# The next batch's turned x: loaded from DRAM and normalised along its columns, instead of turned on TensorE

## The reference

```python
x = x + jnp.tanh(g_xattn[0]) * xattn(_layernorm(x, axis=-1), ctx_1024, ctx_1024, Wq, Wk, Wv, Wo)
x = x + jnp.tanh(g_ffn[0]) * ffn(_layernorm(x, axis=-1), router_w, w1, w2)

def _layernorm(x, axis=-1, eps=1e-05):
    m = jnp.mean(x, axis=axis, keepdims=True)
    v = jnp.var(x, axis=axis, keepdims=True)
    return (x - m) / jnp.sqrt(v + eps)
```

## Time and profile before

| | us |
|---|---|
| median of three runs | 1805.26 (1804.03 to 1808.17) |
| the profiled execution | 1803.87 |
| its span, first to last instruction | 1802.1 |
| PE busy | 1687.2 (94%) |
| DVE busy | 1418.2 (79%) |
| ACT busy | 1288.7 (72%) |
| POOL busy | 539.6 (30%) |

### The profile page before, as it was taken

The page is one execution under the profiler, slowest core; times in us unless marked ns, Lnnn a source line. Parts: engine busy times, 40 slices in busy tenths (PEclk is TensorE's granted clock), DMA queues, the critical chain, the costliest instruction groups (busy, mean ns, idle before and its releaser), DMA issues.

```text
span 1802.1 us, 31795 instructions
## 1 busy us (share of the span) xinstructions
PE 1687.2 (94%) x10074; PEld 905.6 (50%) x10074; DVE 1418.2 (79%) x2293; ACT 1288.7 (72%) x3653; POOL 539.6 (30%) x821
## 2 busy tenths in 40 slices
PE   8999999999999989999999998888899999999997
PEld 5223333333333323333333332214899999999997
DVE  7999999999999999999999999997444444444442
ACT  5999999999999999999999999997111111111111
POOL 3331252352243225235223422213222222222222
PEclk9999999999999999999999999999999999999999
DMA  8546225513711731461272163319322222222222
GB/s 233 127 126 179 70 65 143 148 40 104 199 46 51 189 97 47 133 182 40 76 192 62 59 158 88 134 69 297 92 36 38 35 35 37 36 38 35 35 36 28
DMA packets 128247, 172.90 MB, mean 96 GB/s; under 512 B 14496, under 2 KB 105760, under 8 KB 128128
## 3 DMA queue, kind: packets, MB, share of 16 engines
q1 hardware_dynamic: 113152, 150.51, 30.4%
q0 software_dynamic: 14144, 20.44, 6.5%
q10 hardware_dynamic: 832, 0.53, 0.1%
HBM read 117.96 MB, written 53.47 MB: 95 GB/s over the span
## 4 chain that ended last, share of the span: by engine, by line
PE 37%; ACT 26%; DVE 20%; issue 10%; POOL 4%; DMA 2%; SPq 0%; POOLq 0%; DVEq 0%; ACTq 0%
ACT w_all L921 24%; DVE negmax L1102 14%; PE scores L1495 14%; PE scores L1508 13%; PE scores L724 3%; PE acc L737 3%; POOL routed_rows L1302 2%; DVE resid L997 1%; ACT w_all L866 1%; PE spare L587 1%; DMA out<-row_t,gate_token 1%; POOL vz L1325 1%; PE spare L581 1%; DVE rz L1088 1%; PE spare L1485 1%
## 5 line engine op out<-in xcount | busy, mean ns | idle before, releaser
L921 ACT ACTIVATE w_all<-scores,negmax 128x512 f32<-128x512 f32 (+1 forms) x1664 | 1127.6, 751 | 24.3 <-DVE negmax L1102 18.7
L1102 DVE TENSOR_REDUCE negmax<-scores 128x2 f32<-128x1024 f32 (+1 forms) x832 | 1002.6, 1216 | 63.9 <-PE scores L724 56.2
L724 PE MATMUL scores<-q_stack,w_all 128*128 128x512 bf16 (+1 forms) x1664 | 501.4, 383 | 49.9 <-ACT w_all L921 47.8
L921 ACT ACTIVATION_READ_ACCUMULATOR w_all<-scores,negmax 128x1 f32 (+1 forms) x1664 | 449.0, 270 | 0.0
L737 PE MATMUL acc<-w_all,vz 128*32 128x512 f32 (+1 forms) x3328 | 443.2, 605 | 3.0 <-POOL vz L1325 2.8
L1541 ACT ACTIVATE projections<-scores 128x512 f32<-128x512 f32 x142 | 84.9, 598 | 445.0 <-PE scores L1495 445.0
L724 PEld LDWEIGHTS scores<-q_stack,w_all 128*128 128x128 bf16 (+1 forms) x1664 | 115.3, 99 | 524.5 <-ACT w_all L921 391.9
L1325 POOL TENSOR_TENSOR vz<-w_all,rz 128x68 f32<-128x68 f32 (+1 forms) x416 | 125.2, 301 | 787.8 <-DVE rz L1088 762.1
L1495 PEld LDWEIGHTS scores<-row_t,q_stack 128*128 128x128 f32 x2272 | 264.4, 192 | 6.8 <-issue 1.9
L1495 PE MATMUL scores<-row_t,q_stack 128*128 128x128 f32 x2272 | 265.6, 275 | 1.7 <-DVE row_t L1568 1.7
L1508 PE MATMUL scores<-room,projections 128*128 128x256 f32 x1136 | 256.8, 379 | 0.0
(11 more groups left out here) (215 smaller groups left out, 1044.0 us busy)
## 6 DMA issues: line engine op xcount, KB each, us to landing
w_all<-k_parts SPq DMA_DIRECT2D x248, 200.1 KB, 3.5
w_all<-in_w SPq DMA_DIRECT2D x16, 1024.0 KB, 10.0
q_stack<-q_parts SPq DMA_DIRECT2D x248, 64.0 KB, 3.2
k_parts<-parts SPq DMA_DIRECT2D x42, 300.0 KB, 2.8
w_all<-in_ctx_t SPq DMA_DIRECT2D x7, 1601.0 KB
parts<-routed SPq DMA_DIRECT2D x71, 129.0 KB
q_parts<-parts SPq DMA_DIRECT2D x14, 384.0 KB, 3.5
routed<-pad_row SPq DMA_DIRECT2D x8, 645.0 KB
```

The costliest lines, as they stand in the source:

```text
L724: mm = pe.matmul(scores[0:r, 2 * (u % SLOTS) + j % 2, :], k_stacks[g][:, j, lt * P:lt * P + r], q_stack[:, g, j, :], start=True, stop=True)
L921: e = act.activation(probs[0:r, s % RING, j, :], scores[0:r, 2 * (u % SLOTS) + j % 2, :], ACT.Exp, bias=negmax[0:r, u % 4, j % 2:j % 2 + 1 ...
L1102: dve.tensor_reduce(negmax[0:r, u % 4, :], scores[0:r, 2 * (u % SLOTS):2 * (u % SLOTS) + 2, :], AX.X, ALU.max, negate=True).then_inc(negma ...
```

## The change

The host gives the kernel x a second time, with channels in rows (`in_x_t`), and SP loads a batch of it into `x_t` (for batch 1 at the start, later for the batch after next, behind part q 1). The statistics are still taken by DVE from `x_in`. Behind the inverse deviation, SP stores the mean and the inverse deviation of the 512 tokens into a small DRAM tensor (`x_stats`, 2 x 512), waits for both to land, and loads its 4 KB into every partition, over `x_in`, whose rows aren't wanted any more. POOL subtracts and multiplies in `x_t` itself, a half of the channels at a time, now in steps 20 to 23. The fills `x_turn` of steps 27 and 28 are gone, in batch 0's table too; batch 0's own x is still turned as before. `x_in` is reloaded when POOL has finished.

```diff
-    27: ("next", "x_turn", 0), 28: ("next", "x_turn", 1), 29: ("cur", "o_turn", 1), 31: ("next", "q", 0),
+    29: ("cur", "o_turn", 1), 31: ("next", "q", 0),
...
+SHIFT_X = 20
...
+    x_turned = x_t_in.rearrange("b (k p) n -> b p k n", p=P)
+    x_stats = room[:, 0, :].rearrange("p (s n) -> p s n", s=2)
...
+        def spread_x_stats(it):
+            b = it.b
+            sp.wait_ge(rstd_step, 2 * (b + 2))
+            for s, stat in ((0, mv1[:, :, 0]), (1, rstd1[:, 1, :])):
+                sp.dma_start(x_stats_dram[s].rearrange("(t p) -> p t", p=P), stat, allow_slow_non_contiguous=True).then_inc(x_stats_stored, 16)
+            wait_apart(sp, x_stats_stored, 32 * (b + 1), passed_sp)
+            sp.dma_start(x_stats[:, :, :], x_stats_dram.partition_broadcast(P)).then_inc(x_stats_in, 16)
+
         def load_x(it):
 
-            sp.wait_ge(fill_taken, it.made("x_turn", 1))
+            sp.wait_ge(xn_ready, 2 * (it.b + 2))
             sp.dma_start(x_in[:, :, :], x_rows[it.b + 2]).then_inc(x_loaded, 16)
...
+            sp.wait_ge(early_ready, EARLY.index(("q", 1)) + 1)
+            sp.dma_start(x_t[:, :, :], x_turned[1]).then_inc(x_t_loaded, 16)
...
                 for c in ORDER[0:KCHUNK]:
+                    if b == 0 and c == KC + KCHUNK - 1:
+                        spread_x_stats(it)
                     store_parts(it, c)
...
                 for c in ORDER[KCHUNK:2 * KCHUNK]:
+                    if b > 0 and c == KC + KCHUNK + 1:
+                        spread_x_stats(it)
                     store_parts(it, c)
...
                 store_parts(it, 1)
+                if it.ahead:
+                    sp.wait_ge(fill_ready, it.made("q", 1))
+                    sp.dma_start(x_t[:, :, :], x_turned[b + 2]).then_inc(x_t_loaded, 16)
...
-            if name == "x_turn":
-
-                pe.wait_ge(xn_ready, 2 * (b + 2))
-                mm = turn_x(spare, i)
-            elif name == "q":
+            if name == "q":
+                if i == 0 and 0 in halves:
+                    pe.wait_ge(xn_ready, 2 * (b + 2))
                 mm = project_q(spare, i, halves)
...
-            elif name == "x_turn":
-                act.wait_ge(fill_ready, it.made(name, i))
-                act.copy(x_t[:, i, :], spare[:, :]).then_inc(fill_taken, 1)
...
-                if it.next and s in (CENTRE_X, CENTRE_X + 1):
-                    by_row(ALU.subtract, x_in, x_in, mv1[:, :, 0], s - CENTRE_X).then_inc(centred1, 1)
-                if it.next and s in (CENTRE_X + 2, CENTRE_X + 3):
+                if it.next and s in (SHIFT_X, SHIFT_X + 1):
+                    k = s - SHIFT_X
+                    if k == 0:
+                        wait_apart(pool, x_t_loaded, (b + 1) * 16, passed_pool)
+                        pool.wait_ge(x_stats_in, (b + 1) * 16)
+                    pool.tensor_tensor(x_t[:, k, :], x_t[:, k, :], x_stats[:, 0, :], ALU.subtract).then_inc(centred1, 1)
+                if it.next and s in (SHIFT_X + 2, SHIFT_X + 3):
+                    k = s - SHIFT_X - 2
                     pool.wait_ge(centred1, 2 * (b + 1))
-                    by_row(ALU.mult, x_in, x_in, rstd1[:, 1, :], s - CENTRE_X - 2).then_inc(xn_ready, 1)
+                    pool.tensor_tensor(x_t[:, k, :], x_t[:, k, :], x_stats[:, 1, :], ALU.mult).then_inc(xn_ready, 1)
```

More of the change, by code:

```diff
@@ L203, in rows_of, with attention_and_routing @@
     return min(P, L - lt * P)
-def attention_and_routing(nc, ctx, block, keep, x, ctx_t, g_xattn, g_ffn, wq_t, wk_t, wv_t, wo_t, router_t,
-                          w1, w2, out, routed, q_parts_dram, k_parts_dram):
+def attention_and_routing(nc, ctx, block, keep, x, x_t_in, ctx_t, g_xattn, g_ffn, wq_t, wk_t, wv_t, wo_t, router_t,
+                          w1, w2, out, routed, q_parts_dram, k_parts_dram, x_stats_dram):
     ident, tri, ones, pad_row, plan = (keep[name] for name in ("ident", "tri", "ones", "pad_row", "plan"))
@@ L356, in attention_and_routing @@
     centred1 = sem("centred1")
+    x_t_loaded = sem("x_t_loaded")
+    x_stats_stored = sem("x_stats_stored")
+    x_stats_in = sem("x_stats_in")
     centred2 = sem("centred2")
@@ L1113, in run @@
                     f = it.fill(s)
-                    if f and f[0] not in ("v", "own_v", "x_turn") and p == (f[0] in ("q", "k")):
+                    if f and f[0] not in ("v", "own_v") and p == (f[0] in ("q", "k")):
                         take(it, *f)
@@ L1627, in _, with flamingo_block @@
         pool.wait_ge(added, NBLK * 16)
-def flamingo_block(nc, x, ctx_t, g_xattn, g_ffn, wq_t, wk_t, wv_t, wo_t, router_t, w1, w2, out):
+def flamingo_block(nc, x, x_t, ctx_t, g_xattn, g_ffn, wq_t, wk_t, wv_t, wo_t, router_t, w1, w2, out):
     routed = nc.dram_tensor("routed", (SPARE + BLK, ROW), F32, kind="Internal").ap()
@@ L1633, in flamingo_block @@
     k_parts_dram = nc.dram_tensor("k_parts", (2, 3, D, L), BF16, kind="Internal").ap()
+    x_stats_dram = nc.dram_tensor("x_stats", (2, N), F32, kind="Internal").ap()
     with ExitStack() as ctx:
@@ L1642, in flamingo_block @@
         block = ctx.enter_context(nc.Block())
-        attention_and_routing(nc, ctx, block, keep, x, ctx_t, g_xattn, g_ffn, wq_t, wk_t, wv_t, wo_t, router_t, w1, w2,
-                              out, routed, q_parts_dram, k_parts_dram)
+        attention_and_routing(nc, ctx, block, keep, x, x_t, ctx_t, g_xattn, g_ffn, wq_t, wk_t, wv_t, wo_t, router_t, w1, w2,
+                              out, routed, q_parts_dram, k_parts_dram, x_stats_dram)
         experts(nc, ctx, block, keep, routed, out)
@@ L1658 @@
         ("x", np.ascontiguousarray(inputs["x"])),
+        ("x_t", turned(inputs["x"])),
         ("ctx_t", turned(inputs["ctx_1024"])),
```

## The result

The changed kernel takes 1860.13 us (median of 4 runs, 1858.83 to 1862.59) where the kernel before took 1805.36 beside it (4 runs, 1804.03 to 1808.17). The ratio is 1.0304, with a 95% interval of 1.029 to 1.0317: 3% slower, 55 us, far above the range. The profiled execution has a span of 1857.0 us.

A forecast was written before the change was run, and what follows sets the result against it. ACT and DVE were taken to bind at once beside the removed copies. A gain of 2.4 us, with the trip and other transfers at nought, took the median 1805.26 to 1802.9 (predicted 1803.0); range 1800.3 to 1811.5 us.

The forecast's parts named there:

- the landing of the second store: Statistics' trip through DRAM before step 20: landing 2.5 to 4.6 us after issue, 2.8 taken, in a trip of 7.3.
- Rival C: Statistics stores: 512 stores of 4 bytes twice take some 6 us instead of 2.8; 1810 and above; chance 0.08.
- Rival B: Load spreading 4 KB over 128 partitions: half rate, 3.1 us longer, trip 10.4 us, time 1809.9; chance 0.12.
- The room: POOL's wait at step 20: nothing lost up to a trip of 8.9 us after rstd; 7.3 expected, cost 0.
- The slope: POOL's wait at step 20: from a trip of about 9.4 us on, each microsecond costs one, seven times.
- The gain: Fills removed from steps 27 and 28: 0.3 us a batch for six batches plus 0.6 in batch 0, 2.4 us.
- rival A: Fills removed from steps 27 and 28: ACT alone binds, all 6.6 us arrive, time 1798.7; chance 0.11.
- rival D: Around 423 us: DVE gives nothing back, its waits being PE's own; time 1805.3; chance 0.17.
- POOL: Two subtractions and two multiplications moved to steps 20 to 23: 1.04 us each, hidden there, no cost unless vz is late.
- Other transfers: SP's queue: the turned x load adds 0.6 us of issue and some 3 us of transfer, x_in reloads earlier; all nought.

The follow-up runs named there:

- the packed one: The changed kernel with mean and inverse deviation side by side on each partition, stored by one transfer of 128 rows of 32 bytes: 1802.9 us, ratio 0.9989.
- the run with 8 bytes: The changed kernel with its 1024 writes of 4 bytes 8 bytes apart in DRAM, the spreading load reading a row of ctx_t: 1801.8 us.
- the kernel two steps later: The changed kernel with POOL's four operations on the turned x starting at step 22 instead of 20: 1816.37 us, ratio 1.0057.
- the run ordered by partition: The changed kernel storing means and variances as 1024 adjacent 4-byte writes in partition order, the spreading load reading ctx_t: 1843.6 us.
- the removal alone: The kernel before, without PE's transposes and ACT's copies of steps 27 and 28 and nothing in their place: 1802.27 us, ratio 0.9988.

## Why the prediction was wrong

**The step that failed** is the landing of the second store: "between 2.5 and 4.6 after its issue ... I take 2.8". It measured 8.7 to 12.0. The bounds came from a store of 300 KB in long rows, and the text says beside them that no row of a tiny store exists and that one of 4-byte pieces could be slower, "which I leave to the upper end". The upper end was then 4.6, the slowest of the long-row stores: an unknown below the evidence was given the bound of the evidence. An honest upper bound did not follow from any row of the trace, and the range and the chances should have said so.

**Rival C** had the right place and the right sign, with a chance of 0.08 and a price of 6 us for the landing, half of what it is. Its condition reads well by the table: the landing is the stores' alone. What it said of the cause, that there are 512 stores of 4 bytes twice, is only half right, since as many of them 16 to 512 bytes apart land in 2 to 4 us.

**Rival B** is refuted. The spreading load of 512 KB from one 4 KB row landed in 4.0 to 5.2 us in the changed kernel and in 3.6 to 3.8 in the packed one, where the prediction took 3.8 and rival B 3.1 more. The half rate that the Trainium skill gives for reads at the same large pitch ("DMA: Bandwidth & Descriptors", section "Latency and other measured facts") did not show: the window of the load, which holds a store of k parts too, stands at 188 GB/s (417 to 421 us above).

**The room was right.** The text has nothing lost up to a trip of 8.9 us and a microsecond for each from 9.4 on. In the run with 8 bytes, trips of 8.7 and 8.8 us lost nothing and those of 9.1, 9.2, 9.3 and 9.5 lost 0.1, 0.3, 0.4 and 0.5, all with a full clock. So the point lies at 8.9 and the slope is one, as it is in the kernel two steps later. In batch 0, with its 0.3 us of further room, a trip of 9.0 us lost nothing there and one of 12.0 with a full clock lost 2.8 in the run ordered by partition. POOL's timeline of the trip of 9.5 us (batch 3 of the run with 8 bytes) shows the mechanism as the text has it:

```profile
547.82 0.30 POOL L1343 TENSOR_TENSOR vz<-w_all,rz 128x68 f32<-128x68 f32 x1 [1.72 <-DVE rz L1106]
550.24 1.27 POOL L1381 TENSOR_TENSOR room<-room 128x512 f32<-128x512 f32 x1 [2.11 <-DMA room<-in_ctx_t]
551.46 0.30 POOL L1343 TENSOR_TENSOR vz<-w_all,rz 128x68 f32<-128x68 f32 x1
```

**The slope was not the whole price.** In batch 2 the trip is 15.54 us, 6.64 beyond the 8.9, and 8.18 were lost. The rest, 1.54 us, is the half clock: it lasts 3.4 us behind PE's restart, and half of that is 1.7. The prediction has no term for it. Over seven batches the losses are 8.2, 9.3, 8.2, 8.4, 8.2, 7.5 and 7.8, together 57.5 (unrounded). The trips beyond 8.9 us make 45.8 of them, and the other 11.7 go with the half clock, for which the same estimate gives 13.2. Less the gain of 2.9, 57.5 makes the 55 us measured.

**The gain was right** in mechanism and nearly in size: 2.9 for 2.4, rival A (6.6) excluded by the removal alone, rival D (nought) too. DVE binds beside the copies, as the earlier trace rows were read.

**POOL** was taken at 1.04 us an instruction and takes 1.27 with a full row as second operand (1.53 with the strided row of the packed version). At steps 20 to 23 this hides, as forecast. At steps 25 to 28 it does not.

**Other transfers** were put at nought, and that was wrong in one place, hidden in the changed kernel by the larger loss. SP's wait for the landing stands ahead of a store of k parts, which ACT needs in batch 0. The text lists the queue behind POOL's wait but not the queue behind SP's. Once POOL's wait was moved later, batch 0 lost 6 to 8 us this way.

## What to carry to other kernels

Here a store's landing was set by where its pieces fall and not by its bytes: before a transfer of small pieces through DRAM is put on a path, lay it out so that each partition writes one run, or leave 64 bytes between the pieces, and spend the copy that this takes. When a trace has no row for an operation, its bound is open at that end; measure it, or give the open end its share of the range. Where a wait is added, list what is queued behind it on every engine that waits, the one that issues the transfers included.

## What the runs showed of the hardware

- 1024 writes of 4 bytes side by side in DRAM land 8.7 to 12.0 us after the issue of the second store; the same writes 64 bytes apart in 2.0 to 2.2, and the same 4 KB as 128 writes of 32 bytes in 1.5. In the slow case the DMA engines show 0.00 of busy time for the last 9 us (408 to 417 us), so the records of transfers don't show the delay; only the waiting instruction does.
- 4 KB spread over 128 partitions by one load (512 KB) land in 3.6 to 5.2 us.
- In a pause of PE of 3.02 us the clock fell to the 1.2 GHz level in one batch, and in one of 3.39 us it stayed full in another of the same run. At the lower level the weighing took 1.94 us for 1.07, and a batch lost about half of the time at that level behind the restart.
- POOL's operation on two full operands of 128x512 takes 1.27 us, where one with a repeated value takes 1.04.
